# Rotary keys of a batch element handled as one 128-row strip tile, table loads in order of use, and zero matmuls ahead of the first projection

## The reference, cut to what matters

```python
q = (hidden_states @ wq).reshape(B, S, H, D)
k = (hidden_states @ wk).reshape(B, S, Hkv, D)
v = (hidden_states @ wv).reshape(B, S, Hkv, D)
q = q * cos + _rotate_half(q) * sin
k = k * cos + _rotate_half(k) * sin
scores = jnp.einsum('bqkgd,bskd->bkgqs', qg, k) * scale
attn = jax.nn.softmax(scores, axis=-1)
out = jnp.einsum('bkgqs,bskd->bqkgd', attn, v).reshape(B, S, E)
...
x = _layernorm(x + _L0_attn_ref(x, ...), axis=-1)
x = _layernorm(x + _L0_ffn_ref(x, ...), axis=-1)
```

## Time and profile before

| | |
|---|---|
| median of 3 runs | 948.05 us (947.54 to 948.25) |
| the profiled execution, its own time | 946.2 us |
| its span, first to last instruction | 944.0 us |
| TensorE busy | 909.5 us (96%) |
| VectorE busy | 761.7 us (81%) |
| ScalarE busy | 720.3 us (76%) |
| GpSimd busy | 263.1 us (28%) |
| mean granted clock of TensorE | 0.984 |

### The profile page before, as it was taken

How to read it: one execution, slowest core, us unless ns; L and a number is a source line. 1 busy time by engine, 2 the same in 40 slices (tenths; PEclk the granted TensorE clock), 3 DMA queues, 4 the chain that set the end, 5 groups by cost and what they waited for, 6 DMA issues and landing times.

```text
span 944.0 us, 15638 instructions
## 1 busy us (share of the span) xinstructions
PE 909.5 (96%) x5520; PEld 467.6 (50%) x5520; DVE 761.7 (81%) x1522; ACT 720.3 (76%) x938; POOL 263.1 (28%) x223
## 2 busy tenths in 40 slices
PE   7688999999999999999999999999999999999995
PEld 3234334344434444343434444444435888888884
DVE  4787899999999999999999999999973456655544
ACT  1356888989898898988998889888887555555564
POOL 5777366110001001001000100400101666656454
PEclk9797999999999999999999999999999999999998
DMA  6797633133131232213313123221110201101001
GB/s 206 205 266 199 140 89 93 44 85 72 44 72 45 58 76 69 51 43 74 82 45 68 49 51 84 68 52 42 33 52 14 69 24 46 45 26 42 24 23 47
DMA packets 44288, 68.85 MB, mean 73 GB/s; under 512 B 12592, under 2 KB 22832, under 8 KB 44208
## 3 DMA queue, kind: packets, MB, share of 16 engines
q1 hardware_dynamic: 43344, 64.67, 26.1%
q0 software_dynamic: 864, 3.15, 1.1%
HBM read 46.80 MB, written 16.25 MB: 67 GB/s over the span
## 4 chain that ended last, share of the span: by engine, by line
PE 86%; issue 4%; POOL 3%; DVE 2%; ACT 2%; DMA 1%; SPq 0%; POOLq 0%; DVEq 0%; ACTq 0%
PE pv_bank L1198 27%; PE ring_bank L1121 25%; PE pair_bank L1256 13%; PE pair_bank L1319 12%; PE pv_bank L1328 3%; PE ring_bank L1328 3%; PE ring_bank L1208 2%; POOL rotated L533 1%; POOL low L522 1%; ACT probs L1048 1%; PE ring_bank L1134 1%; PE ring_bank L1223 1%; POOL rotated_k L533 0%; DVE v_all L863 0%; DVE low L714 0%
## 5 line engine op out<-in xcount | busy, mean ns | idle before, releaser
L1048 ACT ACTIVATE probs<-pair_bank 128x1024 f32<-128x1024 f32 x512 | 496.4, 1026 | 68.2 <-PE pair_bank L1256 66.9
L745 DVE TENSOR_REDUCE block_max<-ring_bank 128x1 f32<-128x512 f32 x732 | 469.1, 683 | 33.3 <-PE ring_bank L1121 25.6
L1121 PE MATMUL ring_bank<-k_max,q_sb 48*128 48x512 f32 x1003 | 315.4, 476 | 4.6 <-DMA q_sb<-shift 2.2
L1198 PE MATMUL pv_bank<-probs,v_all 128*32 128x512 f32 x2048 | 273.6, 606 | 0.5 <-ACT probs L1048 0.5
L1121 PEld LDWEIGHTS ring_bank<-k_max,q_sb 48*128 48x128 f32 x1003 | 136.6, 185 | 252.1 <-DVE block_max L745 125.3
L1256 PE MATMUL pair_bank<-q_sb,k_sb 50*128 50x512 f32 x1024 | 204.4, 415 | 0.9 <-ACT probs L1048 0.9
L608 POOL TENSOR_TENSOR attn<-attn,inv_rows 128x1024 f32<-128x1024 f32 x7 | 16.7, 2379 | 489.2 <-DMA inv_rows<-inv_d 489.2
L906 DVE SCALAR_TENSOR_TENSOR hid<-pair_bank,up_s,silu 128x512 f32<-128x512 f32 x64 | 47.9, 748 | 86.7 <-ACT silu L1088 86.7
L1256 PEld LDWEIGHTS pair_bank<-q_sb,k_sb 50*128 50x128 f32 x1024 | 101.5, 187 | 32.8 <-ACT probs L1048 14.4
L650 POOL TENSOR_TENSOR hid_l<-hid,hid_h 128x512 fp32r<-128x512 f32 x64 | 82.9, 1295 | 87.8 <-ACT hid_h L1074 87.2
L742 DVE CUSTOM_DVE_ANT_0 above<-ring_bank,above 128x512 f32<-128x512 f32 x136 | 93.8, 692 | 10.5 <-ACT above L992 6.7
(11 more groups left out here) (126 smaller groups left out, 873.4 us busy)
## 6 DMA issues: line engine op xcount, KB each, us to landing
q_sb<-q_parts SPq DMA_DIRECT2D x64, 128.0 KB, 3.3
k_max<-k_parts SPq DMA_DIRECT2D x32, 192.0 KB, 3.8
attn<-xT SPq DMA_DIRECT2D x8, 512.0 KB, 5.5
q_parts<-high SPq DMA_DIRECT2D x16, 256.0 KB, 3.5
q_parts<-low SPq DMA_DIRECT2D x16, 256.0 KB, 3.6
q_sb<-q_parts SPq DMA_DIRECT2D x64, 64.0 KB, 3.4
k_sb<-k_parts SPq DMA_DIRECT2D x32, 128.0 KB, 2.7
attn<-pv_sb SPq DMA_DIRECT2D x128, 32.0 KB
```

What stands on the lines that cost most here:

```text
L745: dve.reduce_max(block_max[half % 2][:, col:col + 1], bank, axis=AX.X).then_inc(ring_used, 1)
L1048: act.activation(probs[t % 2][:, 2 * pr:2 * pr + 2, :], pair_bank[pr][:], ACT.Exp, scale=D ** -0.5).then_inc(probs_ready, 1)
L1121: pe.matmul(bank, q_sb[k][rows, i, qt * P:(qt + 1) * P], k_max[k // QH][rows, kind * CH:(kind + 1) * CH], start=True, stop=True).then_inc( ...
L1198: ins = pe.matmul(pv_bank[32 * j:32 * j + 2 * D, :], v_all[:, head, t, :], probs[t % 2][:, 2 * (j % 2) + j // 2, :], start=(t == 0), stop= ...
```

## The change

Four things change, all in the first stage:

- **Keys and values in strips.** `wkv` holds keys and values once (128 columns instead of 192). In each block `project_kv` makes four matmuls of 32 columns per k: two strips of key rows into `k_bank`, two of value rows into `v_bank`; the next block fills the other strips. After two blocks `k_bank` holds the keys of the whole batch element in 128 rows, and `rotary_k`, the rotation, `high_k`, `low_k` and `copy_v_rows` run once per batch element on 128 rows instead of once per block on 64. The key store becomes two DMAs per part.
- **The key gap on TensorE.** A matmul of the rotated keys with a 128x64 matrix of +1 and -1 (`key_signs`, made from the identity) gives the difference in a PSUM bank of the ring; `gap_h` is then ScalarE's and `gap_l` VectorE's for all four batch elements.
- **Loads in the order of use.** `wq` first, then tokens of block 0, the query tables in two halves, `wkv`, the key tables; each consumer has its own semaphore. The tokens of block m + 3 are asked for after the first store of block m (block 5's: behind `first_loads`), the twelve loads of block 6 stand ahead of that block's stores, and the key store stands behind the second query store.
- **Three matmuls of zeros.** VectorE clears `by_cos[2]` first, and TensorE multiplies it by itself three times into `v_bank` before it waits for `wq`.

```diff
-            load_x(0)
-            for dst, src in ((wq_sb, wq), (wkv_sb, wkv)):
-                sp.dma_start(dst[:], src.rearrange("(k p) n -> p k n", p=P)).then_inc(proj_loaded, 16)
-            for dst, src in ((cos_sb, cos), (sinq_sb, sin_q)):
-                sp.dma_start(dst[:], src).then_inc(consts_loaded, 16)
+            sp.dma_start(wq_sb[:], wq.rearrange("(k p) n -> p k n", p=P)).then_inc(wq_loaded, 16)
+            load_x(0)
+            load_q_tables(0)
+            sp.dma_start(wkv_sb[:], wkv.rearrange("(k p) n -> p k n", p=P)).then_inc(wkv_loaded, 16)
+            for dst, src in ((cosk_sb, cos_k), (sink_sb, sin_k)):
+                sp.dma_start(dst[:], src).then_inc(k_tables_loaded, 16)
             load_x(1)
-            for dst, src in ((cosk_sb, cos_k), (sink_sb, sin_k)):
-                sp.dma_start(dst[:], src).then_inc(consts_loaded, 16)
+            load_q_tables(1)
             load_x(2)
...
+            def projections(b, first, last):
+                for c in range(2):
+                    m = 2 * b + c
+                    if last and c == 0:
+                        load_kv(0, 0)
+                        load_k(k_max, 0, 1, kmax_loaded, sp)
+                        load_q(0, QH, sp)
+                    store_q(m, 0)
+                    if c == 0 and not first:
+                        store_gap(b - 1)
+                    if m + 3 < BLOCKS and m != 2:
+                        load_x(m + 3)
+                    if last and c == 1:
+                        load_shift(0, 0, taken_through((0, "split")))
+                    store_q(m, 1)
+                    if m == 2:
+                        first_loads()
+                        load_x(m + 3)
+                    if m == 4:
+                        load_q(0, 1, sp)
+                    if c == 1:
+                        store_k(b)
...
             for m in range(BLOCKS):
                 b, c = divmod(m, 2)
                 rotate(m, 0)
-                if m:
-                    low_of(m - 1, 2)
-                if c == 0 and b > GAPS:
-                    key_gap(b - 1)
+                if c == 0 and b:
+                    low_of_k(b - 1)
                 rotate(m, 1)
                 if m >= FIRST:
                     low_of(m, 0)
                 low_of(m, 1)
-                if c == 0 and b > GAPS:
-                    gap_low(b - 1)
-                rotate(m, 2)
-            low_of(BLOCKS - 1, 2)
-            key_gap(B - 1)
-            gap_low(B - 1)
+                if c == 1:
+                    rotate_k(b)
+            low_of_k(B - 1)
...
-            dve.wait_ge(consts_loaded, 16 * 4)
+            dve.memset(by_cos[2][:], 0.0).then_inc(warm_ready, 1)
...
-            pe.wait_ge(proj_loaded, 16 * 2)
+            pe.wait_ge(warm_ready, 1)
+            for n in range(WARM):
+                pe.matmul(v_bank[:], by_cos[2][:, 0:P], by_cos[2][:], start=True, stop=True)
+            pe.wait_ge(wq_loaded, 16)
...
-                c = m % 2
-                if k == 0 and m > 1:
-                    pe.wait_ge(parts_ready, PARTS[-1] * (m - 1))
-                    pe.wait_ge(v_rows_ready, m - 1)
-                ins = pe.matmul(kv_bank[c][:], wkv_sb[:, k, HKV * D * c:HKV * D * (c + 2)], x_in[m][:, k, :], start=(k == 0), stop=(k == KE - 1))
+                b, c = divmod(m, 2)
+                if k == 0 and m == 0:
+                    pe.wait_ge(wkv_loaded, 16)
+                if k == 0 and c == 0 and b:
+                    pe.wait_ge(k_parts_ready, K_PARTS * b)
+                    pe.wait_ge(v_rows_ready, b)
+                for strip in range(4):
+                    a, other = strip // 2, strip % 2 != c
+                    col = (HKV * D if other else 0) + a * STRIP
+                    rows = slice(strip * STRIP, (strip + 1) * STRIP)
+                    ins = pe.matmul((v_bank if other else k_bank)[rows, :], wkv_sb[:, k, col:col + STRIP], x_in[m][:, k, :], start=(k == 0), stop=(k == KE - 1))
...
+            def make_gap(b):
+
+                pe.wait_ge(signs_ready, 1)
+                pe.wait_ge(k_rot_ready, b + 1)
+                bank = free_bank(("gap", b))
+                pe.matmul(bank[0:HKV * D, :], key_signs[:].rearrange("p a x -> p (a x)"), rotated_k[:], start=True, stop=True).then_inc(ring_ready, 1)
```

More of the change, by code:

```diff
@@ L236, in layer @@
                 for key in early[n, h]:
[L237 removed]
+                    place(key, key[0] if key[0] in ("v", "gap") else "max" if key[1] == "split" else ("above" if blocks(key[0], key[1] // 4)[key[1] % 4][1] == 2 else "max"))
         early_entries = len(readers)
@@ L353, in first_loads @@
             def first_loads():
-                for slot in range(2 * QK):
-                    sp.wait_ge(stored[slot], stores(slot))
+                for slot in range(4):
+                    sp.wait_ge(stored[slot], 16 * 2)
+                sp.wait_ge(k_stored[0], 16 * 2 * K_STORES)
                 sp.wait_ge(gap_stored, 16 * 2)
@@ L389, in store_k, with store_q @@
-            def store_k(part, b, cols, buf, done):
-                dst = k_parts[b, part * D:(part + 1) * D, :, cols].rearrange("r h t -> (r h) t")
-                sp.dma_start(dst, buf[0:HKV * D, :].bitcast(fp32)).then_inc(done, 16)
+            def store_q(m, j):
+                b, c = divmod(m, 2)
+                slot = 2 * c + j
+                cols = slice(c * CH, (c + 1) * CH)
+                for part, buf, ready, count in ((0, high, hi_ready, 2 * m + j + 1), (1, low, lo_ready[j], m + 1)):
+                    sp.wait_ge(ready, count)
+                    dst = q_parts[H * b:H * (b + 1), part, j * HALF:(j + 1) * HALF, cols]
+                    sp.dma_start(dst, buf[slot][:].bitcast(fp32)).then_inc(stored[slot], 16)
@@ L428, in _ @@
             store_gap(B - 1)
-            for slot in range(2 * QK):
-                sp.wait_ge(stored[slot], stores(slot) * B)
+            for slot in range(4):
+                sp.wait_ge(stored[slot], 16 * 2 * B)
+            for c in range(2):
+                sp.wait_ge(k_stored[c], 16 * 2 * K_STORES * (B // 2))
             sp.wait_ge(gap_stored, 16 * 2 * B)
@@ new lines, in low_of, with rotate_k @@
+                if b:
+                    pool.wait_ge(stored[slot], 16 * 2 * b)
+                pool.wait_ge(hi_ready, 2 * m + j + 1)
+                pool.tensor_tensor(low[slot][:], rotated[j][:], high[slot][:].bitcast(fp32), ALU.subtract).then_inc(lo_ready[j], 1)
+            def rotate_k(b):
+                pool.wait_ge(k_parts_ready, K_PARTS * (b + 1))
+                if b:
+                    pool.wait_ge(k_lo_ready, b)
+                    pool.wait_ge(ring_ready, places["gap", b - 1] + 1)
+                pool.tensor_tensor(rotated_k[:], by_cos[2][:], by_sin[2][:], ALU.add).then_inc(k_rot_ready, 1)
```

258 lines of the change are left out of this document (124 added, 134 removed).

## The result

The changed kernel takes 955.34 us (median of 5 runs, 953.12 to 956.66) beside 948.05 us for the kernel before on the same chip (5 runs, 946.61 to 948.62): a ratio of 1.0072, 95% interval 1.0056 to 1.0089. It is slower by 7.3 us where 7.2 us less were forecast, and lies outside the range of 935.5 to 945.8. The profiled execution took 954.26 us with a span of 952.4.

The account below looks back on a forecast made before the run. TensorE bounds attention, the feed-forward and blocks 5 to 7, so only first-stage waits could shrink: 6.4 us up to the last key/value pass plus 0.8 after it, 7.2 off 948.05, giving 940.9; range 935.5 to 945.8.

Parts of the forecast that it names:

- What is late next: the first loads: Loads before block 5: with landing times as before, 4.5 and 6 us, block 5 starts with a lead of 9.0 us.
- the four rivals: More gained, 0.15; zeros useless or first blocks late, 0.13; strips one after another, with other losses 0.11; no change, 0.05.
- rival 2: Zeros do nothing, or first blocks run later with landings 1 to 2 us late: 943.5 to 946, chance 0.13.
- rival 3: In key/value steps the four strips run one after another: 955 to 980, chance 0.11 together with other losses.
- The start: Before the first rotation: zeros bring the clock up at about 7.3, and GpSimd starts at 11.2, 3.5 us earlier.
- Blocks 0 to 4: First-stage blocks: first rotations of blocks 1 to 4 at 16.6, 23.6, 29.9, 35.6; a key/value step takes 1.06 us.
- The first loads: Before block 5: gap's low part issued at 29.3, landed at 33.8 when the loads start; TensorE begins block 5 at 43.3.
- The clock at block 5: After a 6.6 us idle stretch TensorE's clock falls to half; the price is taken as 2.4 us.
- Blocks 5 to 7: TensorE-bound last blocks: net +0.2 us, the last key/value pass ends at 74.2, 6.4 us earlier.
- The end: From last key/value pass to attention: TensorE needs 8.5 to 9.3 us instead of 9.8, taken as 0.8 saved.
- Attention: The stage after the first scores: its instructions are left alone, so it stays at 602 us.

Follow-up runs that it names:

- the start alone: Kernel before with only the new load order, halved query tables, separate semaphores, the clear and zero matmuls: 942.11 us, ratio 0.9942 to the kernel before.
- wide stores: Changed kernel with all key stores cut into pieces of 32x512, eight DMAs per batch element instead of four: 939.45 us, ratio 0.9908 to the kernel before.
- the version with eight narrow ones: Changed kernel with eight key stores per batch element, cut along the tokens to 2x32x256: 955.45 us, ratio 1.0087 to the kernel before.

## Why the prediction was wrong

**The step that failed** is in "What is late next: the first loads", where the forecast says "Same DMA load, same times". It took landings of 4.5 us for the gap's low part and 6 us for tokens from the kernel before, and put no term for the changed key store itself, whose landing the first loads also wait for. The bytes were the same, but the store had gone from 64x512 to 2x32x512, and the DMA engines ran at 0.12 to 0.13 for 4 us behind it, where the forecast took their load for the 0.9 to 0.98 of the earlier trace rows. The first loads left at 41.17 instead of 33.8. None of the four rivals has this mechanism. The nearest was rival 2's later landings, priced at 1 to 2 us under a full load; it was 7 us, at an almost idle one. That the result of 955.34 is the low end of rival 3 is chance, since its strips run side by side.

Point by point:

- *The start.* Right in mechanism, slightly undersized. Zeros at 1.44 to 6.0, the first projection at 6.07 with the clock up (the forecast had it up at 7.3), the first rotation at 10.62 (forecast 11.2). On the kernel before, the start alone is worth 5.1 us by the medians and 3.2 by the profiled spans, against 3.5.
- *Blocks 0 to 4.* Right: the first rotations came at 17.1, 22.8, 29.0 and 35.2 where 16.6, 23.6, 29.9 and 35.6 were forecast. The four strips of a key/value step run side by side (passes of 0.59 to 0.62 us that start within 0.03 us of each other); rival 3 is excluded.
- *The first loads.* The failed step in the changed kernel. With wide stores the sum is near (34.02 and 43.21 against 33.8 and 43.3), but by luck: the gap's low part was issued at 31.17 and not at 29.3, since eight key stores stand ahead of it, and landed in about 2.8 us and not 4.5. The two errors cancel. (The 2.7 us that the forecast names for the shorter token load is 6.0 - 3.2 = 2.8; it stands in no sum.)
- *The clock at block 5.* Right that it falls to half. The price was 2.4; with wide stores four passes took 3.48 instead of 1.88, and the clock was back after that: 1.6.
- *Blocks 5 to 7.* The last key/value pass of the wide version ended at 72.3 (forecast 74.2). The clock gives 0.8 of the difference. The other 1.1 isn't the key/value steps, which became 0.07 us shorter each, as forecast; most of it lies in block 7, which took 8.9 us (from 63.35) instead of the 10.3 of the earlier trace rows. Why is not shown.
- *The end.* Undersized. With wide stores the maxima matmul just ahead of the first scores (before, the one that waited for the shift and to which the forecast's 9.8 counts) started 81.78 - 72.3 = 9.5 us after the last key/value pass, where 8.5 to 9.3 were forecast. The last gap matmul came at half clock and took 1.97. VectorE's low part behind it then held the first scores, which came 1.44 us after that matmul, instead of 0.56 (91.00 - 90.44). So the end cost 10.9 us up to the scores, where it was 10.4 before and 0.8 less was forecast. The forecast said that the gap's store is needed only later, which is so, but the first scores stand behind VectorE's reading of the bank. In the changed kernel SyncE was late as well (shift issued at 88.36), so that the stores set the end there.
- *Attention* was to stay at 602. With wide stores the same pattern stands at 684.24, 601.0 us behind the first scores, and at 691.96 - 91.00 = 601.0 before; in the changed kernel it is 606.9.

The errors on blocks 5 to 7 and on the end cancel: 939.45 with wide stores is within 1.5 us of the forecast's 940.9, in part by luck. What the forecast lacked was one term, of 15.5 us, for an edit that it didn't price at all.

## What to carry to other kernels

When a change merges stores or loads, price the new access pattern and not only bytes and issues: look at the outermost dimension of both sides, and split a DMA along a dimension of 2 rather than let it lead. A low DMA share with transfers queued, at a flat multiple of 1/16, is the sign in the profile, and a DMA of the ordinary kind with an issue of 3 to 4 us behind the guilty one is the second (issues up to 1.96 us stand in the trace of before too). And a narrow DMA costs least where nothing urgent waits for it or for what is queued behind it: with four in front of the loads that gate block 5 it started 6.9 us late (50.06 against 43.21), with two 1.8 (44.99).

## What the runs showed of the hardware

- Four stores of 128 KB that use two of the DMA engines also delay the others on their queue: the next issue took 3.65 us, and 0.53 with wide stores in their place; that of `wo` 4.14 and 4.28, and 0.43 (5.63 for four stores in the version with eight narrow ones). Stores queued behind land late as well. The chain of waits that the profile builds for the changed kernel names one of them as its longest piece ahead of the first loads:

```profile
34.75 6.35 DMA q_parts<-low
```

  The program doesn't wait for that store, though; what the first loads wait for are the key stores (3.7 us) and the gap's (1.9 us), which end at about the same time.

- A filled wait keeps the clock. Matmuls whose result nobody reads held TensorE's granted clock at 1.00 through a wait of 7 us, in which it otherwise fell to 0.50. At the start, with three matmuls of zeros ahead of it, the first projection takes 3.60 us, and 6.03 without them (both with wide stores).
- Why the issue itself is held up, and not only the landing, is not shown by any run.
